# Windowed attention block with GDN on one core: the transposes of a round gathered in one run of 64-row tiles

## The reference, cut to what matters

```
x = transpose(x, (0, 2, 3, 1))                  # 4 images, 128 x 128 pixels, C = 96
y = roll(ln(x, norm1), (-4, -4)) cut in 8 x 8 windows -> (windows, 64 tokens, 96)
q, k, v = heads(y @ qkv_w.T + qkv_b)            # 6 heads of 16; q * 16 ** -0.5
attn = softmax(q @ k.T + mask)                  # mask: -100 across the rolled border
out = (attn @ v) @ proj_w.T + proj_b            # back from windows, roll (4, 4)
x = x + out
h = gelu(ln(x, norm2) @ w1.T + b1)              # hidden 384
x = x + (h @ w2.T + b2)
x = x * rsqrt((x * x) @ gamma_eff.T + beta_eff) # GDN over the 96 channels
```

## Time and profile before

| | |
|---|---|
| median of 3 runs | 1819.56 us (1818.24 to 1821.19) |
| profiled execution, its own time | 1816.74 us |
| its span | 1814.5 us |
| granted clock of PE, mean | 0.995 |
| busy: PE, DVE, ACT, POOL | 97%, 92%, 87%, 86% of the span |

### The profile page before, as it was taken

How to read it: one execution, slowest core, us unless ns; L and a number is a source line. 1 busy time by engine, 2 the same in 40 slices (tenths; PEclk the granted TensorE clock), 3 DMA queues, 4 the chain that set the end, 5 groups by cost and what they waited for, 6 DMA issues and landing times.

```text
span 1814.5 us, 78584 instructions
## 1 busy us (share of the span) xinstructions
PE 1764.4 (97%) x31203; PEld 1344.6 (74%) x31203; DVE 1677.5 (92%) x4637; ACT 1587.7 (87%) x2700; POOL 1553.4 (86%) x1661
## 2 busy tenths in 40 slices
PE   5899999999999999999999999999999999999997
PEld 3677777777777777777777777777777777777774
DVE  5799999999999999999999999999999999999985
ACT  2799999998999899989899999899989989998895
POOL 4488999988898888998898898898888889898883
PEclk9899999999999999999999999999999999999999
DMA  2111222122122122222121221221221221221211
GB/s 57 24 42 39 49 52 42 44 52 44 43 52 45 42 52 42 45 51 43 44 50 36 52 51 37 51 51 36 52 51 35 53 50 34 54 50 33 46 34 27
DMA packets 215143, 81.17 MB, mean 45 GB/s; under 512 B 116118, under 2 KB 214780, under 8 KB 214780
## 3 DMA queue, kind: packets, MB, share of 16 engines
q1 hardware_dynamic: 214218, 76.04, 19.2%
q10 hardware_dynamic: 562, 0.11, 0.0%
HBM read 25.75 MB, written 25.17 MB: 28 GB/s over the span
## 4 chain that ended last, share of the span: by engine, by line
PE 95%; DVE 1%; issue 1%; ACT 1%; DMA 0%; SPq 0%; POOL 0%; POOLq 0%; DVEq 0%; ACTq 0%
PE mm_bank L952 50%; PE score_banks L1013 7%; PE turn_bank L945 7%; PE turn_bank L938 6%; PE mm_bank L986 6%; PE pv_bank L1056 5%; PE score_banks L1033 5%; PE score_banks L1042 3%; PE mm_bank L1069 3%; PE mm_bank L1066 2%; PE score_banks L1021 1%; SPq L373 0%; PE mm_bank L1116 0%; DMA k_block<-k 0%; DMA x_ext<-in_x 0%
## 5 line engine op out<-in xcount | busy, mean ns | idle before, releaser
L452 POOL TENSOR_TENSOR hidden_lo<-hidden,hidden_hi 128x512 fp32r<-128x512 f32 x378 | 480.9, 1285 | 0.0
L539 ACT ACT_TABLE_LOAD x253 | 324.6, 1283 | 4.5
L452 POOL TENSOR_TENSOR attended_lo<-attended,attended_hi 96x512 fp32r<-96x512 f32 x127 | 163.8, 1290 | 111.0 <-DVE attended_hi L834 111.0
L808 DVE TENSOR_REDUCE row_max<-score_banks 128x8 f32<-128x512 f32 x384 | 241.4, 684 | 17.8 <-PE score_banks L1021 9.9
L582 ACT ACTIVATE probs<-shifted 128x512 f32<-128x512 f32 x384 | 236.4, 629 | 20.1 <-DVE shifted L816 13.2
L816 DVE TENSOR_TENSOR shifted<-score_banks,row_max 128x512 f32<-128x512 f32 x384 | 250.8, 680 | 0.0
L615 ACT ACTIVATE hidden<-mm_bank 128x512 f32<-128x512 f32 x381 | 228.6, 600 | 20.5 <-PE mm_bank L952 2.2
L447 POOL TENSOR_SCALAR hidden_hi<-hidden 128x512 fp32r<-128x512 f32 x378 | 228.5, 615 | 4.0 <-ACT hidden L615 3.8
L765 DVE BATCH_NORM_STATS2 stats<-turn_bank 128x6 f32<-128x96 f32 x1024 | 192.8, 250 | 30.2 <-PE turn_bank L938 25.8
L594 ACT ACTIVATE probs_t<-score_banks 128x512 f32<-128x512 f32 x384 | 214.5, 594 | 5.8 <-PE score_banks L1033 4.0
L468 POOL TENSOR_TENSOR x_sq<-x 96x512 f32<-96x512 f32 x126 | 130.7, 1037 | 73.7 <-DVE x L846 66.2
(11 more groups left out here) (144 smaller groups left out, 4815.3 us busy)
## 6 DMA issues: line engine op xcount, KB each, us to landing
x_ext<-in_x SPq DMA_DIRECT2D x128, 192.0 KB, 3.1
k_block<-k SPq DMA_DIRECT2D x768, 32.0 KB
out<-o_ext SPq DMA_DIRECT2D x128, 192.0 KB, 2.7
w_raw<-in_w_t SPq DMA_DIRECT2D x1, 144.0 KB
w<-in_w_t SPq DMA_DIRECT2D x1, 144.0 KB
qkv_raw<-in_qkv_t ACTq DMA_DIRECT2D x1, 108.0 KB
ident_sb<-in_ident SPq DMA_DIRECT2D x1, 64.0 KB, 2.3
q_quadrants<-in_qmask SPq DMA_DIRECT2D x3, 1.0 KB
```

The lines of the kernel that those rows point to most:

```text
L452: nc.gpsimd.tensor_tensor(lo, whole, hi, ALU.subtract).then_inc(is_split, 1)
L539: nc.scalar.preload_act_table_set(name)
L808: nc.vector.tensor_reduce(row_max[:, g, :], group_scores(g), op=ALU.max, axis=AX.X)\
```

## The change

- PE does all transposes of a round except `turn_in` in one piece, `turn_run`: the 24 of the probabilities and 16 for the two norms (each 128-token chunk in two halves), all in tiles of 64 rows, with the two row halves of the array taking turns and writing different banks. The two banks of the norms become one tensor of two banks (`turn_banks`); row half 0 writes bank 0 and row half 1 bank 1 for both norms, so `split_y2` also waits for norm 1's copy, and `turn_in` for both norms' readers.
- The projection is one full fp32 matmul. The cast on DVE, the subtraction on POOL and the split weights are gone; `attended` has no second buffer, so `divide` waits for the projection of the half before.
- `y1` is kept with the rows 0 to 3 of all 16 windows ahead of the rows 4 to 7. ACT's copy of norm 1 is then two instructions of 256 columns, POOL's two steps on it read one piece without gaps, and the matmuls of q and k read it as 8 windows of two pieces of 32 tokens.
- PE, DVE, ACT, POOL and the shared banks get new orders. DVE still writes the output (`outputs`).

The core of the diff:

```diff
 MM_ITEMS = [
+    ("k", QK, k_ready, 1, 1),
+    ("den", DIVIDE, log_den_made, 1, 1),
     ("sum", ATTEND - 1, log_sum_made, 1, 1),
-    ("k", QK, k_ready, 1, 1),
+    ("v", ATTEND, v_ready, 1, 1),
     ("q", QK, q_ready, 1, 1),
-    ("den", DIVIDE, log_den_made, 1, 1),
     ("mlp2", SETTLE, x3_ready, 1, 1),
-    ("v", ATTEND, v_ready, 1, 1),
     ("proj", PROJECT, x2_ready, 1, 1),
...
+def turn_windows(A, m, p, n):
+
+    half = slice(TOKENS * n, TOKENS * (n + 1))
+    bank, first = (n, (m * PAIRS + p) * TOKENS) if m < 2 else (2, (n * PAIRS + p) * TOKENS)
+    return nc.tensor.transpose(score_banks[:, bank, first:first + TOKENS],
+                               probs[half, m, p, :, :], ident_sb[half, half])
+
+def turn_normed(A, ln, n, r):
+
+    half, first = slice(64 * r, 64 * (r + 1)), ln * 256 + n * 64
+    made = nc.tensor.transpose(turn_banks[0:DIM, r, first:first + 64],
+                               y_tok[ln][half, chunks_of(A)[n], :], ident_sb[half, half])
...
+def turn_run(H):
+
+    A, norm1, norm2 = H + ATTEND, H + TURN_OUT, H + MLP
+    if has(A):
+        pe.wait_ge(probs_ready, GROUPS * A + 2)
+        for m in range(2):
+            for p in range(PAIRS):
+                for n in range(2):
+                    made = turn_windows(A, m, p, n)
...
+        pe.wait_ge(probs_ready, GROUPS * A + 3)
+    if has(norm1):
+        pe.wait_ge(normed[0], norm1 + 1)
+    if has(norm2):
+        pe.wait_ge(normed[1], norm2 + 1)
+    for p in range(PAIRS):
+        if has(A):
+            made = turn_windows(A, 2, p, 0)
+            if p == PAIRS - 1:
+                made.then_inc(first_windows_turned, 1)
+        if has(norm1):
+            turn_normed(norm1, 0, p, 1)
+    for p in range(PAIRS):
+        if has(norm1):
+            turn_normed(norm1, 0, p, 0)
+        if has(norm2):
+            turn_normed(norm2, 1, p, 1)
+    if has(A):
+        pe.wait_ge(first_windows_turned, A + 1)
+    for p in range(PAIRS):
+        if has(norm2):
+            turn_normed(norm2, 1, p, 0)
+        if has(A):
+            made = turn_windows(A, 2, p, 1)
...
 def project(A, a):
-    pe.wait_ge(attended_split, A + 1)
+    pe.wait_ge(attended_ready, A + 1)
     mm_wait("proj", A)
-    in_parts(mm_bank("proj", A)[0:DIM, :], wproj_hi[:, :], wproj_lo[:, :],
-             attended_hi[:, :], attended_lo[:, :]).then_inc(proj_made, 1)
+    nc.tensor.matmul(mm_bank("proj", A)[0:DIM, :], wproj[:, :], attended[:, :],
+                     start=True, stop=True).then_inc(proj_made, 1)
...
 def y_copy(A, a, ln):
...
+    for r in range(2):
+        dst = by_window[:, r * HALF_WINDOWS:(r + 1) * HALF_WINDOWS, :, :]
+        src = normed_columns(0)[:, :, r, :].rearrange("c q (n x) -> c n q x", x=WIN)
+        made = nc.scalar.activation(dst, src, ACT.Copy)
...
 in_parts(mm_bank("k", A)[0:DIM, :], wk_hi[:, :], wk_lo[:, :],
-             half_of(y1_hi[rows, unit_slot(a), :], a), half_of(y1_lo[rows, unit_slot(a), :], a))\
+             y1_windows(y1_hi, a), y1_windows(y1_lo, a))\
...
 def steps(run, H):

     run(scores, ATTEND)
+    run(project_k, QK)
+    run(denominators, DIVIDE)
     run(sum_probs, ATTEND - 1)
     run(times_v, ATTEND - 1)
-    run(project_k, QK)
+    run(project_v, ATTEND)
     run(project_q, QK)
-    run(turn_out, MLP, 1)
-    run(denominators, DIVIDE)
+    turn_run(H)
     for n in range(HID_CHUNKS):
         run(mlp_down, SETTLE, n)
-    run(project_v, ATTEND)
-    run(turn_out, TURN_OUT, 0)
     run(project, PROJECT)
-    run(turn_two_groups, ATTEND)
     run(turn_in, TURN_IN, 0)
-    run(turn_last_group, ATTEND)
     run(mlp_up, MLP, 0)
+    run(turn_in, PROJECT, 1)
     run(mlp_up, MLP, 1)
-    run(turn_in, PROJECT, 1)
     run(mlp_up, MLP, 2)
```

More of the change, by code:

```diff
@@ L303, in in_windows, with y1_rows, y1_windows @@
             return flat.rearrange("c (n r w) -> c n r w", r=WIN, w=WIN)
-        def ln_rows(flat, a):
-            rows = TOKENS // 2
-            return flat.rearrange("c (n t) -> c n t", t=TOKENS)[:, :, (a % 2) * rows:(a % 2 + 1) * rows]
+        def y1_rows(tile, a):
+            return half_of(tile[:, unit_slot(a), :], a)
+        def y1_windows(tile, a):
+            by_window = tile[:, unit_slot(a), :].rearrange("c (h n t) -> c n h t", h=2, t=TOKENS // 2)
+            return by_window[:, half_windows(a), :, :]
         def half_of(tile, a):
@@ L427, in set_rows @@
             def set_rows():
-                for hi, lo in ((y2_hi, y2_lo), (attended_hi, attended_lo), (x3_sq_hi, x3_sq_lo)):
+                for hi, lo in ((y2_hi, y2_lo), (x3_sq_hi, x3_sq_lo)):
                     nc.gpsimd.memset(hi[DIM:DIM + 1, :].bitcast(f32), 1.0).then_inc(rows_set, 1)
@@ L651, in steps @@
                 run(gelu, MLP, 2)
-                run(load_tables, MLP - 1, "natural_log_exp_and_others")
             rounds(steps)
@@ L789, in split_y2 @@
                 dve.wait_ge(y_ready[1], A + 1)
-                nc.vector.tensor_tensor(half_of(y2_lo[0:DIM, :], a), turn_banks[1][0:DIM, :],
-                                        half_of(y2_hi[0:DIM, :], a), ALU.subtract).then_inc(y2_split, 1)
+                dve.wait_ge(y_ready[0], min(A - MLP + TURN_OUT + 1, HALVES))
+                lo, hi = (half_of(tile[0:DIM, :], a).rearrange("c (q r t) -> c q r t", r=2, t=64)
+                          for tile in (y2_lo, y2_hi))
+                nc.vector.tensor_tensor(lo, normed_columns(1), hi, ALU.subtract).then_inc(y2_split, 1)
             def v_blocks(A, a):
@@ L823, in divide @@
                 dve.wait_ge(pv_made, A + 1)
+                wait(dve, proj_made, A)
                 for m in range(HEAD_PAIRS):
@@ L860, in steps @@
                 run(max_scores, ATTEND, 1)
+                run(shift_scores, ATTEND, 0)
                 run(max_scores, ATTEND, 2)
-                run(normalise, MLP, 1)
-                run(shift_scores, ATTEND, 0)
-                run(divide, PROJECT)
-                run(normalise, TURN_OUT, 0)
-                run(round_attended, PROJECT)
                 run(shift_scores, ATTEND, 1)
                 run(shift_scores, ATTEND, 2)
+                run(normalise, TURN_OUT, 0)
+                run(normalise, MLP, 1)
+                run(v_blocks, ATTEND)
+                run(divide, PROJECT)
+                run(outputs, DIVIDE)
+                run(split_y2, MLP)
                 run(second_residual, SETTLE)
-                run(split_y2, MLP)
-                run(v_blocks, ATTEND)
                 run(first_residual, PROJECT)
-                run(outputs, DIVIDE)
                 run(statistics, TURN_IN, 0)
@@ L930, in turn_in @@
                     pe.wait_ge(x2_ready, A + 1)
-                wait(pe, (y_ready[0], y2_split)[ln], A)
+                before = A - (TURN_IN, PROJECT)[ln]
+                wait(pe, y_ready[0], min(before + TURN_OUT + 1, HALVES))
+                wait(pe, y2_split, min(before + MLP + 1, HALVES))
                 for n, c in enumerate(chunks_of(a)):
@@ L1102, in mlp_down @@
                     made.then_inc(mlp2_made, 1)
-            def last_project():
-                pe.wait_ge(attended_ready, FINAL + 1)
-                mm_wait("proj", FINAL)
-                nc.tensor.matmul(mm_bank("proj", FINAL)[0:DIM, :], wproj[:, :], attended[:, :],
-                                 start=True, stop=True).then_inc(proj_made, 1)
             def last_mlp_down(A):
@@ L1161, in _ @@
             late(sum_probs, FINAL)
-            late(turn_out, FINAL - 1, 1)
+            turn_run(FINAL - 1 - MLP)
             late(denominators, FINAL - 3)
-            last_project()
+            late(project, FINAL)
             for n in range(HID_CHUNKS):
@@ L1169, in _ @@
             late(mlp_up, FINAL - 1, 1)
-            late(turn_out, FINAL, 1)
+            turn_run(FINAL - MLP)
             late(mlp_up, FINAL - 1, 2)
```

111 lines of the change are left out of this document (42 added, 69 removed).

## The result

The changed kernel takes 1768.84 us in the median of 4 runs (1768.05 to 1775.52), the kernel before 1820.38. The ratio is 0.971, 95% interval 0.969 to 0.974. The profiled execution has a span of 1766.9 us, 47.6 less than before.

A forecast was written before the change was run, and what follows sets the result against it. PE, busy 97% of the span, was taken as the bound. PE's terms gave 0.31 us a round, less 0.07 and 0.04 is 0.20, times 128 = 26 us: 1791, plus 2.8, 1794 us; range 1780 to 1806, given 0.65.

The forecast's parts named there:

- Turns: PE's transposes: 1.76 us a round go out, 40 tiles by 0.032 plus one exit of 0.13 come in, saving 0.35.
- the slower rivals: Cases with a slower kernel: mixed tiles not overlapping 0.08, weight loads hiding nothing 0.02, windowed reading of y1 0.03, among others.
- the one of mixed tiles: Rival: PE's 24 tiles of probabilities and normed tokens do not overlap, 0.77 us more a round, 1893 us; chance 0.08.
- Projection: PE's projection: 0.87 us goes out, one full fp32 matmul of two 0.44 passes comes in at 0.88, costing 0.01.
- Openings and entries: PE's block openings and tile entries and exits around q, v and the sums in the new order: costs 0.03 us.
- the ring: DVE from projection to normalisations, then PE from mixed tiles back to projection: 12.99 us, or 13.35 as read; 0.07 counted.
- The allowance of 0.04 for ACT: PE's sums wait 0.04 us a round for ACT's copy of k, which stands behind the table load.
- The round: Net saving per round from scores to scores on PE: 0.31 - 0.07 - 0.04 = 0.20 us, times 128.
- The prologue and the tail keep their work: Start and end of the kernel, outside the rounds: claimed unchanged, with a few tiles in place of transposes.
- POOL: POOL's chain from second residual to denominators' input: 4.3 us against 4.7 available; PE waits if the residual is over 0.4 late.

## Why the prediction was wrong in size

The way was right, the time was below the range. By its steps:

- **Turns: 0.35.** Right: the run takes 1.41 us, as forecast to the hundredth, and mixed tiles cost the same as like ones. Of the slower rivals that this excludes, the one of mixed tiles had been given 0.08.
- **Projection 0.01.** Right. The matmul is two passes of 0.43 us in every place. The 0.95 in the old place is 0.86 and the entry into the tiles, which the prediction had priced at 0.09.
- **Openings and entries 0.03.** Right but for the 0.07 that k with the denominators take more than forecast, 1.63 us for 1.56. Some 0.05 of it is the sums' wait for the copy of k.
- **The turn-in of x: left at its old 0.39.** This is the largest step that failed. The prediction priced the blocks that moved, but not this one, whose neighbours moved: it stood behind tiles and ahead of plain fp32, and stands now behind plain fp32 and ahead of fp32r. It takes 0.27. By single starts its first transpose takes 0.085 for 0.138 and its last 0.028 for 0.082. So PE's own work came out at 13.00 us with the wait taken off and at 13.05 with it, where the prediction had 13.10.
- **The allowance of 0.07 for the ring.** This step failed too. The ring had been worked out at 12.99 us, shorter than PE's own work, and was charged all the same. The changed kernel and the one with the extra DVE instruction put it 0.06 us under the round, where it had been worked out, and there it costs nothing.
- **The allowance of 0.04 for ACT.** Right: the sums wait some 0.05 us for the copy of k. But it is not the table load that decides when the copy starts, as the prediction had it; the load has ended 0.03 us before k's own product lets the copy go.
- **The round.** 0.36 measured for 0.20. The turn-in gives 0.12 of this and the ring 0.07; ACT's wait and the small differences take 0.03 back. Times 128 that is 20 of the 25 us between forecast and measurement.
- **The range.** Its lower end, 1780 us, already had both allowances at nothing. What took the time below it are the 0.05 of PE's own work, 6 us, and some 5 us beyond the rounds' medians: 2 from the first scores, the longer rounds and the tail together, and the 2.8 us that were added from the profiled execution to the median, where the changed kernel's two differ by 0.2.
- **The edges.** "The prologue and the tail keep their work" was wrong on both sides. The tail is 7.7 us longer. 3.8 of these are table loads that one moved line brings, shown by taking them out; the rest goes with a lower granted clock, whose cause is open. The distances beyond the medians lose 8.9 us in the profile; 4.3 of these are in the first four, where the moved line and the clock both act and were not separated. The rest are fewer stalls within runs of small tiles that the trace puts down to issue: before, nine of 0.3 to 0.8 us; in the changed kernel, three of 0.2 to 0.6. Why there are fewer of those was not settled. That these gains and the longer tail nearly cancel is luck.
- **POOL** is waited for nowhere in a middle round, as forecast.

## What to carry to other kernels

When the bound engine is full, the price of a block lies in its neighbours: read each block as the distance to the next one's start, and price a moved block by a place in the trace that has the same kinds of block on both sides. Do the same for a block that stays while its neighbours move. A ring or chain that is shorter than the bound engine's own work costs nothing, however close it is; it belongs in the upper end of the range and not in the sum. And a line moved across the edge of a loop has to be followed through the first and the last turn.

## What the hardware showed unexpectedly

- Transposes in two alternating row halves go at 0.032 us for 64 rows, so 128 rows take 0.065, against 0.109 from start to start at full height in the same place. Without the tiles nothing of the gain is left.
- The last transpose of a full-height block takes 0.03 us up to an fp32r matmul and its full step (0.08 of x, 0.11 of `y_tok` and `probs`) up to plain fp32. Behind tiles the first one takes some 0.05 us more than elsewhere.
- The small 32-column tiles start every 0.013 us (64 in 0.81).
- Behind the same two waits of over 1 us in the warm-up the clock was at its lower level for 17 us in one profile and stayed up in another of the same kernel. That the waits bring it down is not shown.
- A wait can be there without a name in the timeline: that for the copy of k shows only in distances, 0.38 us for 0.33.
